# A gated linear attention block with an FFN: last k sums through PSUM, outer products all on GpSimd, PSUM banks permuted, output statistics moved

## The reference

```python
q, k, v = (x @ W).reshape(B, L, 16, 8)             # Wq, Wk, Wv
gk = log_sigmoid(x @ Wgk1 @ Wgk2 + bgk2) / 16
state = state * exp(gk)[..., None] + v[..., None] * k[..., None, :]   # per token
out_t = einsum('bhvk,bhk->bhv', state, q)
out = (out - mean) / sqrt(var + 1e-5) * gamma + beta
x1 = layernorm(x + (out * silu(x @ Wg)) @ Wout)    # "x2" in the kernel
h = silu(x1 @ w1 * s1) * (x1 @ w2 * s2)            # 128 -> 512
h = gelu(h @ h1 * s); h = gelu(h @ h2 * s)         # 512 -> 512, twice
out = layernorm(x1 + h @ w3 * s3)                  # 512 -> 128
```

## Time and profile before

| | |
|---|---|
| median of 3 runs | 186.07 us |
| the profiled execution's own time | 184.29 us |
| its span on the core | 182.5 us, 2765 instructions |
| TensorE busy | 161.6 us (89%), 802 matmuls |
| VectorE busy | 148.0 us (81%), 306 |
| ScalarE busy | 111.6 us (61%), 179 |
| GpSimd busy | 113.1 us (62%), 96 |

### The profile page before, as it was taken

The page is one execution under the profiler, slowest core; times in us unless marked ns, Lnnn a source line. Parts: engine busy times, 40 slices in busy tenths (PEclk is TensorE's granted clock), DMA queues, the critical chain, the costliest instruction groups (busy, mean ns, idle before and its releaser), DMA issues.

```text
span 182.5 us, 2765 instructions
## 1 busy us (share of the span) xinstructions
PE 161.6 (89%) x802; PEld 123.2 (68%) x802; DVE 148.0 (81%) x306; ACT 111.6 (61%) x179; POOL 113.1 (62%) x96
## 2 busy tenths in 40 slices
PE   0898988999879997999999699999996998999980
PEld 0755756868657774878778477577773885887770
DVE  1499989979889997998999997989999794874062
ACT  4554889992157453478683547667635669959421
POOL 8997898879609688670677678608685320670032
PEclk9999999999999999999999999999999999999998
DMA  3999900000000000000000001000000120000102
GB/s 115 313 389 416 381 18 0 0 4 0 4 0 0 2 0 0 4 2 0 0 0 0 0 0 57 0 0 0 4 0 0 48 83 0 4 0 0 57 4 63
DMA packets 6496, 8.97 MB, mean 49 GB/s; under 512 B 562, under 2 KB 5203, under 8 KB 5971
## 3 DMA queue, kind: packets, MB, share of 16 engines
q1 hardware_dynamic: 5906, 5.93, 10.2%
q0 software_dynamic: 576, 2.88, 4.1%
HBM read 7.76 MB, written 1.05 MB: 48 GB/s over the span
## 4 chain that ended last, share of the span: by engine, by line
PE 37%; DVE 13%; ACT 4%; issue 3%; POOL 3%; POOLq 0%; DVEq 0%
PE ffn L608 6%; PE ffn L617 6%; PE att L530 4%; PE ffn L586 2%; DVE y L1083 2%; PE att L655 2%; PE ffn L674 2%; PE att L643 2%; PE att L514 2%; DVE y L1087 2%; PE ffn L667 2%; PE ffn L591 2%; PE att L515 2%; DVE o_acc L1090 1%; PE att L541 1%
## 5 line engine op out<-in xcount | busy, mean ns | idle before, releaser
L1072 DVE TENSOR_TENSOR_SCAN state<-gate,att 128x512 f32<-128x512 f32 x32 | 38.3, 1208 | 1.5 <-PE att L530 1.5
L366 POOL TENSOR_TENSOR f_lo<-full,f_hi 128x512 fp32r<-128x512 f32 x18 | 23.4, 1315 | 25.9 <-DVE full L1158 18.2
L894 ACT ACTIVATE f_hi<-ffn,vec_cols 128x512 fp32r<-128x512 f32 x24 | 16.6, 690 | 25.1 <-PE ffn L617 24.9
L325 POOL TENSOR_TENSOR u_tok<-kv_tok 128x1024 f32<-128x1024 f32 (+1 forms) x12 | 27.3, 2281 | 1.9 <-DVE o_acc L1090 1.4
L608 PE MATMUL ffn<-f_hi,h_hi 128*128 128x512 f32 x96 | 27.3, 404 | 0.0
L617 PE MATMUL ffn<-f_lo,h_hi 128*128 128x512 f32 x96 | 26.6, 399 | 0.0
L340 POOL TENSOR_TENSOR o_acc<-o_acc,y 128x512 f32<-128x512 f32 x16 | 20.7, 1296 | 7.9 <-DVE y L1083 7.7
L1083 DVE TENSOR_TENSOR y<-att,state 128x512 f32<-128x512 f32 x32 | 21.1, 670 | 0.0
L608 PEld LDWEIGHTS ffn<-f_hi,h_hi 128*128 128x128 f32 x96 | 17.6, 188 | 4.7 <-ACT f_hi L886 0.9
L617 PEld LDWEIGHTS ffn<-f_lo,h_hi 128*128 128x128 f32 x96 | 17.8, 188 | 4.1
L530 PE MATMUL att<-ident,u_tok 128*128 128x128 f32 x128 | 18.5, 275 | 1.3 <-DVE u_tok L1049 0.9
(11 more groups left out here) (176 smaller groups left out, 357.9 us busy)
## 6 DMA issues: line engine op xcount, KB each, us to landing
h_raw<-in_hT SPq DMA_DIRECT2D x2, 1024.0 KB, 12.5
h_hi<-in_hT POOLq DMA_DIRECT2D x2, 1024.0 KB, 11.9
x_tok<-in_x SPq DMA_DIRECT2D x4, 256.0 KB, 5.8
out<-out_tok SPq DMA_DIRECT2D x3, 256.0 KB, 2.3
w_raw<-in_w12T SPq DMA_DIRECT2D x1, 512.0 KB, 5.5
w_hi<-in_w12T POOLq DMA_DIRECT2D x1, 512.0 KB, 8.8
xT_raw<-in_xT SPq DMA_DIRECT2D x1, 256.0 KB, 2.7
proj_raw<-in_proj SPq DMA_DIRECT2D x2, 128.0 KB, 2.3
```

Source lines behind the costliest of these rows:

```text
L325: nc.gpsimd.tensor_tensor(u_tok[:, j].rearrange("p k (h v) -> p k h v", v=DH), v_b.unsqueeze(1).to_broadcast([P, DH, HEADS, DH]), k_b.unsq ...
L366: nc.gpsimd.tensor_tensor(lo[:, o], full_block(layer, o), hi[:, o].bitcast(F32), ALU.subtract).then_inc(pool_rested, 1)
L894: nc.scalar.activation(hidden[layer][0][:, o], bank[:], ACT.Gelu, scale=scales[:, 1 + layer, o:o + 1]).then_inc(gelu_hi_ready, 1)
L1072: nc.vector.tensor_tensor_scan(state[:, k % 3], gate[:, b], A[2 + k % 2][:], 0.0, ALU.mult, ALU.add).then_inc(scanned, 1)
```

## The change

It does five things.
- Read-out 6 writes its product back into the PSUM bank that held q (`q_bank(b, 6)`), the pair sum reads that and y of k = 7 and writes the bank, and the last sum reads the bank and `o_acc`.
- Tile 1's outer product goes from VectorE to GpSimd. Tiles 0 and 1 of the sequence after next are made at the end of `ffn_middle`, after GpSimd's rests of layer 1; before, tile 0 came at the start of `attention_end`. Tile 2 follows o_rstd, tile 3 r_rstd.
- Layer 2's block o uses bank `F[(0, 2, 3, 1)[o]]` instead of `F[(o + 2) % 4]`. TensorE starts block (2, 0) ahead of `center_o` and block (2, 1) before `project_out`; VectorE makes the rest of (2, 1) before that of (2, 0), and W3's matmuls wait for block (2, 1)'s bank.
- The e mean and variance of the finished sequence go from before VectorE's rest (1, 2) to behind o's variance. e_rstd and e_shift are computed by GpSimd behind o_rstd of the sequence two later, instead of at the end of `ffn_middle`, with the wait for `out_ready` first. ScalarE's `out_normalise` of sequence b - 2 comes behind the first layer-1 gelu of sequence b, and for sequence 1 ahead of the last hidden layer.
- The loops on ScalarE and GpSimd are written out; those on TensorE and VectorE stay.

```diff
-        ON_DVE = [n for n in ALL_BLOCKS if n not in ON_POOL]
+        ON_DVE = [(0, 3), (1, 2), (1, 3), (2, 1), (2, 0), (2, 2), (2, 3)]
+        LAYER_2_BANK = (0, 2, 3, 1)
...
-            return F[((2 * o + 1) % 4, o, (o + 2) % 4)[layer]]
+            return F[((2 * o + 1) % 4, o, LAYER_2_BANK[o])[layer]]
...
             def e_rstd_of(b):
+                pool.wait_ge(out_ready, TILES * b + 1)
                 rstd_of(b, e_var, e_var_ready, e_rstd, e_rstd_ready)
                 pool.wait_ge(e_rstd_ready, b + 1)
                 pool.wait_ge(e_minus_ready, b + 1)
-                pool.wait_ge(out_ready, TILES * b + 1)
                 nc.gpsimd.tensor_tensor(e_shift[:], e_minus[:], e_rstd[:], ALU.mult).then_inc(e_shift_ready, 1)
...
-            def attention_end(a, tiles, follows):
-                if isinstance(a, int) and a == 0:
-                    pool.wait_ge(o_ready, 1)
-                if follows:
-                    outer_products(a + 1, (0,))
+            def attention_end(a, tiles, last_tiles):
                 o_rstd_of(a)
-                if follows:
-                    outer_products(a + 1, tiles)
+                if a >= 2:
+                    e_rstd_of(a - 2)
+                outer_products(a + 1, tiles)
                 r_rstd_of(a)
-                if follows:
-                    outer_products(a + 1, (3,))
+                outer_products(a + 1, last_tiles)
-            def ffn_middle(b, f, follows):
-                if follows:
-                    sum_over_k(b + 1, range(3, DH - 2))
+            def ffn_middle(b, follows):
+                sum_over_k(b + 1, range(3, DH - 2))
                 rest(b, 1, 0)
                 rest(b, 1, 1)
-                if f is not None:
-                    e_rstd_of(f)
+                if follows:
+                    outer_products(b + 2, (0, 1))
...
-            attention_end(0, (1, 2), True)
+            pool.wait_ge(o_ready, 1)
+            outer_products(1, (0,))
+            attention_end(0, (1, 2), (3,))
             first_layer(0, True)
-            ffn_middle(0, None, True)
-            with pool.Fori(0, B - 2) as i:
-                attention_end(i + 1, (2,), True)
-                first_layer(i + 1, True)
-                ffn_middle(i + 1, i, True)
-            attention_end(B - 1, (), False)
+            ffn_middle(0, True)
+            attention_end(1, (2,), (3,))
+            first_layer(1, True)
+            ffn_middle(1, True)
+            attention_end(2, (2,), (3,))
+            first_layer(2, True)
+            ffn_middle(2, False)
+            attention_end(B - 1, (), ())
...
-                    bank_read(b, 1, (o + 2) % OB)
+                    bank_read(b, 1, LAYER_2_BANK[o])
...
             def ffn_out_hi(b, with_lo):
-                bank_read(b, 2, 0)
+                bank_read(b, 2, 1)
...
                 ffn_hidden_rest(f, 1, 3)
+                ffn_hidden(f, 2, 0, with_lo)
                 center_o(a)
                 transpose_o(a)
-                ffn_hidden(f, 2, 0, with_lo)
+                ffn_hidden(f, 2, 1, with_lo)
                 project_out(a)
                 ffn_hidden_rest(f, 2, 0)
-                ffn_hidden(f, 2, 1, with_lo)
                 ffn_hidden_rest(f, 2, 1)
...
-            def first_layer(b, f):
+            def first_layer(b):
...
                 for o in range(OB):
                     ffn_gelu(b, 1, o)
-                out_normalise(f)
+                    if o == 0 and b >= 2:
+                        out_normalise(b - 2)
...
-            with act.Fori(0, B - 2) as i:
-                step(i + 1, i)
-                first_layer(i + 1, i)
+            for b in range(1, B - 1):
+                step(b, b - 1)
+                first_layer(b)
...
             nc.scalar.preload_act_table_set(GELU_SET)
+            out_normalise(B - 3)
             last_gelu_hi(0)
...
-                nc.vector.tensor_tensor(y[:, k % 4], q_bank(b, k)[:], state[:, k % 3], ALU.mult).then_inc(y_ready, 1)
+                dst = q_bank(b, k)[:] if k == 6 else y[:, k % 4]
+                nc.vector.tensor_tensor(dst, q_bank(b, k)[:], state[:, k % 3], ALU.mult).then_inc(y_ready, 1)
             def last_sums(b):
                 dve.wait_ge(y_ready, DH * (b + 1))
-                nc.vector.tensor_tensor(y[:, 3], y[:, 2], y[:, 3], ALU.add).then_inc(pair_ready, 1)
+                pair = q_bank(b, 6)[:]
+                nc.vector.tensor_tensor(pair, pair, y[:, 3], ALU.add).then_inc(pair_ready, 1)
                 dve.wait_ge(summed, (DH - 3) * (b + 1))
                 dve.wait_ge(pair_ready, b + 1)
-                nc.vector.tensor_tensor(o_acc[:], o_acc[:], y[:, 3], ALU.add).then_inc(o_ready, 1)
+                nc.vector.tensor_tensor(o_acc[:], pair, o_acc[:], ALU.add).then_inc(o_ready, 1)
...
                 last_sums(a)
-                if e is not None:
-                    e_mean_and_variance(e)
                 rest(f, 1, 2)
-            def make_x2(a, f, follows):
                 apply_gate(a)
                 o_token_stats(a)
                 rest(f, 1, 3)
                 o_mean_and_variance(a)
-                if follows:
-                    outer_product(a + 1, LATER_U_ON_DVE)
+                if e is not None:
+                    e_mean_and_variance(e)
+            def make_x2(a, f):
                 add_x(a)
+                rest(f, 2, 1)
                 rest(f, 2, 0)
-                rest(f, 2, 1)
                 x2_normalise(a)
```

More of the change, by code:

```diff
@@ L255, in gla_ffn_kernel @@
         G_BANK = (F[1], F[0], F[2], F[3])
-        U_ON_DVE, LATER_U_ON_DVE = (2, 3), 1
+        U_ON_DVE = (2, 3)
         block = ctx.enter_context(nc.Block())
@@ L1306, in _ @@
             with dve.Fori(0, B - 2) as i:
-                make_x2(i + 1, i, True)
+                make_x2(i + 1, i)
                 scan(i + 2, 0)
@@ L1312, in _ @@
                 attention_end(i + 2, i + 1, i)
-            make_x2(B - 1, B - 2, False)
+            make_x2(B - 1, B - 2)
             last = B - 1
```

## The result

The changed kernel took 180.5 us (median of 4 runs, 180.24 to 182.07) beside 185.44 for the kernel before on the same chip (4 runs, 184.79 to 186.28): ratio 0.9755, interval 0.971 to 0.9799. The profiled execution took 180.24 against 184.29 (forecast 181.2), its span 178.4. Medians in this document are of all runs of a kernel; a ratio and its 95% interval leave out, on both sides, runs more than 1.5% above the fastest of their kernel, so a ratio is not always the quotient of two medians.

The account below looks back on a forecast made before the run. VectorE (81%) and TensorE (89%) both nearly full; waits for o_acc, the pair sum and o_rstd bound the stages. 0.57 + 1.20 + 1.31 = 3.1 us off 184.29 gave 181.2, or 183.0 against the median 186.07; range 180.9 to 185.4.

Parts of the forecast that it names:

- the third gain most: Stages 1 to 3, from each sequence's o centering to the next u transposes or FFN input: gains 0.57, 1.20, 1.31 us.
- the last of the sum: Whole kernel: 181.2 us for the profiled execution, which lies 1.8 below the median 186.07, became 183.0 against that median.
- Gate behind centering, 1.36: VectorE's gate on o was taken to follow TensorE's centering by 1.36 us in all three stages.
- e_rstd and its shift, 1.4: GpSimd, stage 2: these two behind o_rstd take 1.4 us, until 110.8, and product 2 then runs until 113.0.
- x2 behind r_rstd, 0.18: Stage 2: r_rstd ends at 114.11 and x2's normalisation starts at 114.29 instead of 115.49.
- The sums at 0.7 us: VectorE's pair and last sums, one input in PSUM, take 0.69 us each unheld by GpSimd; the pair took 1.37 before.
- r_var held to the end of product 2: VectorE, stage 2: r_var, due at 112.18, is held by GpSimd until 113.0, stretched to nearly 1 us.
- rival C: End of kernel: w3_tok's loads behind store 1 land late and TensorE's last matmuls wait, 190.0 us; chance 0.05.
- VectorE's product leaving at nothing: Moving outer product 1 off VectorE gains nothing, since VectorE waits for o_rstd there anyway; bounds nothing to 2.15 us.
- The moved e statistics: VectorE's 6 small e instructions behind o_var are covered under o_rstd's 1.02 us; uncovered they would cost up to 1.0.
- Rival A: GpSimd's products 0 and 1, ahead of o_rstd, take 2.59 us each and come late: 184.5 us; chance 0.18.
- TensorE was put ahead by 1.58 us per stage: Permuted banks: centering 0.64 us earlier plus 0.94 of block (2,0)'s matmuls run in TensorE's hole; x2 still ends stage 2.

Follow-up runs that it names:

- a2_after_again: The changed kernel itself, unedited, run once more beside the kernel before: 181.89 us, ratio 0.9824 to the kernel before.
- d4_loop_edge: The kernel before, VectorE's instructions in the same order, with its loop's boundary put behind o's variance: 184.46 us, ratio 0.9929 to the kernel before.
- d1_sums: The kernel before with the sums through PSUM alone: 183.58 us, ratio 0.9902 to the kernel before.
- b1_e_rstd_last: The changed kernel with GpSimd's e_rstd and shift behind product 3: 180.15 us, ratio 0.973 to the kernel before.
- u5_e_stats_early: The changed kernel with VectorE's mean and variance of the finished row back ahead of the gate: 182.38 us, ratio 0.9827 to the kernel before.
- u2_no_banks: The changed kernel with the old PSUM banks and TensorE's old order: 182.85 us, ratio 0.9821 to the kernel before.
- u4_product1_late: The changed kernel with GpSimd's products 1 and 2 both behind o_rstd: 185.2 us, ratio 0.9936 to the kernel before.
- u1_no_sums: The changed kernel with the sums back in SBUF: 186.5 us, ratio 1.0002 to the kernel before.
- u6_vectore_unrolled: The changed kernel with VectorE's loop over sequences written out: 181.28 us, ratio 0.9741 to the kernel before.

## Why the prediction missed
The direction was right, and the named mechanisms came about; the number was 2.5 us too high. Of the stages the prediction had the third gain most (1.31 against 1.20 in the second); the second did (1.74 against 1.63). The miss has two parts.

**The base, 1.5 us.** The step that failed is the last of the sum, the 1.8 us added to go from the profiled execution to the median. I took the gain off the median of three runs, 186.07, which is 1.8 above the profiled execution. The runs are not scatter around a middle but lie near levels, set in the first 23 us (a2_after_again). 186.07 stood above the lowest one (184.8 against 186.07 and 186.28), the median of the four after on the lowest, which 3 of them held, and that was chance; 183.0 - 181.2 = 1.8 was assumed and 180.5 - 180.24 = 0.26 found. In a2_after_again only 1 of 6 runs was on the lowest, and its ratio, 0.9824, is close to the one forecast (183.0 / 186.07 = 0.9835). The first ratio's interval leaves 0.9835 out; the second's holds it.

**The terms, 1.0 us.** 181.2 forecast for the profiled execution, 180.24 measured; 4.17 gained against 3.08.
- Gate behind centering, 1.36: mis-sized by 0.31, 0.16 and 0.16. It came 1.05, 1.20 and 1.20 us behind. d4_loop_edge shows 0.1 to 0.2 us of the old distance in stages 1 and 2 to be VectorE's loop boundary, which stood at that place and, after the change, stands ahead of add_x, under o_rstd. For stage 3, outside the loop, I took stage 2's value although its own was 1.17 (140.31 to 141.48). Another 0.05 to 0.1 is the centering itself, 1.02 to 1.07 us without a pause of TensorE before it and 1.12 with one.
- e_rstd and its shift, 1.4: 1.21, from o_rstd's end (108.43) to product 2 (109.64). Too dear by 0.19; I had kept the pause that stood between e_rstd and shift when GpSimd's loop was one.
- x2 behind r_rstd, 0.18 as for add_x: 0.03, 112.89 to 112.92. Too dear by 0.15.
- What is left, 0.1 in sum, is small: in stage 3 add_x came 0.11 and not 0.18 behind o_rstd, and x2's rounding on ScalarE 1.79 and not 1.86 behind x2. The centerings were forecast 0.21, 0.64 and 0.65 us earlier within their stages and came 0.20, 0.62 and 0.64; o_var's 2.46 behind the gate stood to 0.01 in all three stages.

**Steps right.** The sums at 0.7 us (d1_sums). r_var held to the end of product 2, though stretched to 0.52 us and not to nearly 1, since product 2 ended sooner than forecast; with e_rstd moved away it is not held and 0.28 us are gained (b1_e_rstd_last). The Trainium skill's rule on two SBUF inputs ("SBUF — State Buffer", section "Who interferes with whom"), which I had put forward for and against, agrees with o_acc's 2.42, e_var's 1.05 and r_var's 0.52 us. out_normalise cost nothing: 1.65 us at 156.25, gelu next at 158.01 with no idle time shown. The loads for w3_tok behind store 1, rival C: SP issued them at 158.71, GpSimd scaled w3_tok from 161.72 to 163.00, 6.2 us before TensorE wanted it.

**Steps not seen.** The prediction put VectorE's product leaving at nothing and o_rstd at 1.02 us; the two are one step, since it was this product that held o_rstd (d4_loop_edge). The moved e statistics were counted at nothing; they are worth 0.68 us (u5_e_stats_early), but the forecast was not wrong by it, since o's path was priced without them. Rival A missed by 0.31 us of slack (106.86 against 107.17); in stage 1 of u2_no_banks, where o comes earlier, o_var was held by product 1. u4_product1_late prices product 1 made late, 3.2 us in all. Permuting the banks is worth 0.80 us in the changed kernel, all of it in stage 3 (u2_no_banks): TensorE was put ahead by 1.58 us per stage, but it isn't what ends stages 1 and 2.

## What to carry to other kernels
VectorE work with two SBUF inputs, however small (e_var: 1.05 instead of 0.16 us), should not meet GpSimd's long multiplications: move one input to PSUM, or move the instruction to where GpSimd waits, and only then load GpSimd further. Write down which of the given times is the profile's own, look whether the runs lie on levels, and give ratio and absolute time apart. When a term comes from a looped stage, look where the loop's boundary lies, and take each stage's own distance where it has one.

## What I had not expected of the hardware
- Which of two conflicting instructions starts first decides, and not alike for both. VectorE's product 0.16 us ahead of GpSimd's power held it (1.93 instead of 1.02); 0.09 us behind it (d4_loop_edge) it ran its usual 1.22 inside the power's 1.01. The Trainium skill, "SBUF — State Buffer", section "Who interferes with whom", has the one that starts first block the other for its whole instruction. GpSimd's multiplications behave so here (product 0 and o_acc in u1_no_sums); its power does not.
- The kernel has levels 1.2 to 1.6 and 2.6 us above its lowest time, made in the first 23 us by TensorE's rate. In the highest the granted clock falls to 0.50. In the middle one it reads 1.00 while 512-column matmuls start 0.43 us apart instead of 0.23; what decides between lowest and middle stays open.
- VectorE's loop cost more than its boundary: 0.74 us went with it in u6_vectore_unrolled, where 0.2 was expected. Waits inside the loop took longer than the same waits written out: 0.13 against 0.04 us from centering to gate, 0.90 against 0.63 from the first transpose to the first scan.
